# Moving two norms between the steps of a fused attention and mixture-of-experts block

## The chip, the cores and the metric

The kernel runs on one core of one Trainium2 chip. The metric is the device time of one execution in microseconds (us); three runs of the kernel before gave 756.25, 756.53 and 757.11. The engines are named as in the profile: PE (TensorE, matrix multiplies), DVE (VectorE), ACT (ScalarE), POOL (GpSimd) and SP (SyncE, which here only issues transfers). Each runs its own instructions in the order written, and they meet at semaphores.

## The reference, cut to what matters

Eight sequences of 256 tokens with 256 features pass through one block. The six modulation vectors come from a small product of c. The attention has 16 query heads and 8 key/value heads of 128 features, rotary embedding, a two-tap causal convolution on keys and values, and a causal window of 128. The expert part has 32 experts, of which each token takes 4, and a shared expert.

```python
h = _layernorm(x, axis=-1) * (1 + ca) + sa          # the input norm
x = x + ga * _L0_attn_ref(h, W_pack, W_o, conv_k, conv_v)
h = _layernorm(x, axis=-1) * (1 + cb) + sb          # the residual's second norm
x = x + gb * _L0_ffn_ref(h, w_norm, w_router, w_gate, w_up, w_down, sw_gate, sw_up, sw_down, w_shared_gate)
```

`_L0_ffn_ref` begins with an RMS norm of its own, then router, experts and shared expert.

## The kernel before, in words

**Pairs and steps.** The sequences are taken two at a time: four pairs (0 to 3) of 512 tokens. The attention is one software pipeline of 128 steps, 32 for each pair. A step n is one head of one sequence. Each engine walks through the same steps (`for n in STEPS`), and in step n it does its share for several heads at once: PE does `scores(n)`, `weighted_v(n - 2)`, `output(n - 3)`, `p_transpose(n - 1)` and `project(n + 4)`; DVE does the masked scores of n, `head_low(n - 2)` (the low part oT_lo of a head's output), in every fourth step `k_conv` (kc), `project(n + 3)` and `normalise(n)` (prob); ACT does `project(n + 3)` (two half copies qsw, or one of v), `head_high(n - 2)`, the exponentials of n and the transposed probabilities of n - 1; POOL does the two rotary operations on the queries and keys. PE's `scores(n)` write one of three PSUM banks and wait for `ot_done` of n - 2, so for `head_low(n - 3)` (lines 1453 to 1465). In every fourth step PE also transposes v (`v_transpose`). In the text "step 7 of pair 2" is n = 2 x 32 + 7.

**Hooks.** At a step's end each engine calls `hooks(n)` (ACT line 635, DVE line 1184, PE line 1558), a table that puts side work of other stages at given steps l of the pair p now in the pipeline. There are two such stages, and both touch the change:

- *The input norm of the next pair*, q = p + 1. DVE takes mean and variance of the four token rows of xin (`prepare_stats`, two calls of two rows each), ACT the reciprocal root (`prepare_norm`, line 517), DVE normalises xin in place (`prepare_norm`, line 976, two calls), PE transposes it in two halves through the PSUM bank XB (`prepare_t`), ACT scales it into hst (`prepare_h`) and rounds the high part (`prepare_hi`), and DVE takes the low part (`prepare_lo`). PE's `project` for the next pair's first head then reads both. `v_transpose` uses the same bank XB, and in group 3 it waits until `prepare_h` is done (line 1473).
- *The end of the pair before*, p - 1 ("post" in the names). DVE gates its attention output (`post_gate`), POOL adds it to the residual (`post_x1`), DVE takes statistics (`post_stats`), ACT the root (`post_std`), DVE the modulated second norm h2 (`post_h2`, four instructions per call, line 1074), ACT its squares and their root (`post_squares`, `post_rms`), DVE the RMS norm (`post_xn`), and PE, ACT and DVE the transposes and the router behind it.

**The load of xin.** `prepare_stats` waits for xin with `ld_xin` (line 968). SP issues that load in `next_x` (line 380) as soon as the pair ahead has been transposed out of xin, but SP's queue is in order too. For pair 2 the load stands behind `pair_loads(0)` and behind three fills of the expert sums with zeros of 2176 KB each (line 424), which come after the modulation rows are done; for pair 3 it stands behind the stores of pair 0 and the loads of pair 1:

```python
            pair_loads(0)
            for d in acc_d:
                sp.dma_start(d.rearrange("(a p) h -> p a h", p=PN),
                             blank[:, 0:H].unsqueeze(1).broadcast_to([PN, B * S // PN + 1, H])).then_inc(st_accz, 16)
            for p in range(NPAIR - 1):
                if p + 2 < NPAIR:
                    next_x(p + 2)
```

After the 128 steps follow the shared expert and the 32 experts, which the change doesn't touch.

## Time and profile before

| What | Value |
|---|---|
| median of three runs | 756.53 us |
| the profiled execution: its own time | 757.21 us |
| the profiled execution: its span, first to last instruction | 755.4 us |
| PE busy | 727.5 us, 96% of the span |
| DVE, ACT, POOL busy | 70%, 62%, 57% |
| mean granted TensorE clock | 0.99 |
| the 128 steps | from 23.2 to about 544 us of the span |

The times in the views count from the span's first instruction. The profiled execution took 757.21 us, 1.8 more than its span, and is one of the slower executions by 0.68 against the median. A busy PE is not a PE at its peak: matmuls overlap, and their ends are modelled. What a row names behind "<-" in brackets is what ended the idle time before it.

### The profile page before, as it was taken

Reading aid. Unit: us, or ns where it says so; the run is one execution under the profiler, and the core shown is the slowest. Engines: PE = TensorE matmul, PEld = TensorE weight load, DVE = VectorE, ACT = ScalarE, POOL = GpSimd, SP = SyncE. Lnnn points to the kernel's source line nnn. Section 1 sums busy time; section 2 is a strip of 40 time slices with the busy share of each in tenths; the row PEclk is TensorE's granted clock in tenths of the full one; section 3 lists DMA queues with packets and bytes.
Section 4 is the critical chain, followed back from the end, with each engine's and each line's share of the span. In section 5 each row is a group of like instructions: output and inputs, shape, how many; then the busy total and the mean of one; then the engine's idle time right before and its main releaser. Section 6 shows DMA issues by size and latency. Waiting matters only on the chain.

```text
span 755.4 us, 12879 instructions
## 1 busy us (share of the span) xinstructions
PE 727.5 (96%) x4144; PEld 624.1 (83%) x4144; DVE 531.0 (70%) x1554; ACT 464.7 (62%) x1273; POOL 429.9 (57%) x339
## 2 busy tenths in 40 slices
PE   8799999999999999999999999999999989999996
PEld 6598889988899998889999888999877857777875
DVE  5898897689876868987686797778664225454383
ACT  5788868777986776788677678777553212222110
POOL 3545445454465588646548864655545507567356
PEclk9999999999999999999999999999999989999998
DMA  8960007600005011000401102040369889996772
GB/s 303 322 139 1 2 0 241 230 0 2 1 1 192 5 49 48 33 1 1 166 2 48 40 28 76 3 168 1 124 166 258 220 267 263 289 228 71 171 226 84
DMA packets 62418, 84.44 MB, mean 112 GB/s; under 512 B 6376, under 2 KB 50293, under 8 KB 62352
## 3 DMA queue, kind: packets, MB, share of 16 engines
q1 hardware_dynamic: 52240, 70.59, 30.4%
q0 software_dynamic: 7680, 8.95, 6.2%
q10 hardware_dynamic: 2432, 4.07, 1.5%
q8 instruction: 34, 0.56, 0.3%
q14 instruction: 32, 0.26, 0.1%
HBM read 54.81 MB, written 33.51 MB: 117 GB/s over the span
## 4 chain that ended last, share of the span: by engine, by line
PE 76%; DVE 12%; ACT 6%; issue 2%; DMA 2%; POOL 1%; ACTq 0%; POOLq 0%; DVEq 0%
PE PJ L1386 22%; PE OUT L1520 9%; PE U L1505 6%; PE U L1465 6%; PE U L1672 5%; PE U L1494 4%; PE U L1464 3%; PE U L1506 3%; PE U L1620 2%; PE U L1386 2%; PE XB L1691 2%; PE OUT L1691 2%; PE OUT L1620 2%; PE XB L1386 2%; ACT U L570 1%
## 5 line engine op out<-in xcount | busy, mean ns | idle before, releaser
L792 POOL TENSOR_TENSOR qsw<-qsw,sinT 128x512 f32<-128x512 f32 x95 | 125.7, 1323 | 167.4 <-ACT qsw L557 166.5
L1017 DVE CUSTOM_DVE_ANT_0 U<-U,mask 128x128 f32<-128x128 f32 (+1 forms) x256 | 86.6, 379 | 50.8 <-PE U L1465 50.4
L570 ACT ACTIVATE U<-U,nmax 128x128 f32<-128x128 f32 (+1 forms) x256 | 100.4, 392 | 32.0 <-DVE nmax L1017 31.5
L1386 PE MATMUL PJ<-hT_hi,w_hi 128*128 128x512 f32 x254 | 110.8, 436 | 1.1 <-issue 1.1
L1386 PE MATMUL PJ<-hT_lo,w_hi 128*128 128x512 f32 x254 | 100.4, 395 | 0.0
L1386 PE MATMUL PJ<-hT_hi,w_lo 128*128 128x512 f32 x254 | 100.2, 394 | 0.0
L796 POOL TENSOR_TENSOR qr<-qr,qsw 128x512 f32<-128x512 f32 x64 | 82.6, 1291 | 29.0 <-DVE qr L1001 28.4
L556 ACT ACTIVATE qsw<-PJ 64x512 f32<-64x512 f32 x96 | 57.1, 594 | 51.7 <-PE PJ L1386 42.3
L803 POOL DMA_INDIRECT slot_rows<-xn,sidx x64 | 64.8, 1012 | 40.8 <-issue 13.1
L1520 PE MATMUL OUT<-wo_hi,oT_hi 128*128 128x256 f32 x256 | 82.9, 324 | 1.4 <-DVE wo_lo L1041 1.2
L1034 DVE TENSOR_TENSOR oT_lo<-U,oT_hi 128x256 fp32r<-128x256 f32 x128 | 54.1, 423 | 37.4 <-ACT oT_hi L577 37.2
L1505 PE MATMUL U<-pT,vN 128*128 128x256 f32 x256 | 77.2, 383 | 1.9 <-ACT pT L589 1.1
L1465 PE MATMUL U<-kc,qr 128*128 128x256 f32 x256 | 76.5, 380 | 0.0
L1027 DVE TENSOR_TENSOR prob<-U,rinv 128x384 f32<-128x384 f32 x128 | 71.3, 557 | 4.4
L896 POOL DMA_INDIRECT expert_sum<-ye,slot_token x32 | 49.7, 1553 | 41.6 <-DVE ye L1327 20.7
L1520 PE MATMUL OUT<-wo_hi,oT_lo 128*128 128x256 f32 x256 | 72.7, 284 | 0.0
L1520 PE MATMUL OUT<-wo_lo,oT_hi 128*128 128x256 f32 x256 | 71.5, 279 | 0.0
L577 ACT ACTIVATE oT_hi<-U 128x256 fp32r<-128x256 f32 x128 | 49.3, 386 | 34.0 <-PE U L1506 26.5
L1464 PEld LDWEIGHTS U<-kc,qr 128*128 128x128 f32 x256 | 46.6, 188 | 24.6 <-DVE oT_lo L1034 9.1
L589 ACT ACTIVATE pT<-U 128x384 f32<-128x384 f32 x128 | 63.4, 496 | 0.7 <-PE U L1494 0.7
L1494 PE MATMUL U<-ident,prob 128*128 128x128 f32 x384 | 62.9, 273 | 0.3 <-DVE prob L1027 0.3
L1464 PE MATMUL U<-kc,qr 128*128 128x128 f32 x256 | 50.8, 280 | 7.8 <-DVE oT_lo L1034 4.0
(227 smaller groups left out, 1837.1 us busy)
## 6 DMA issues: line engine op xcount, KB each, us to landing
wgu<-in_dram SPq DMA_DIRECT2D x32, 352.0 KB, 9.7
expert_sum<-blank SPq DMA_DIRECT2D x3, 2176.0 KB, 17.5
slot_rows<-blank SPq DMA_DIRECT2D x1, 4624.0 KB, 26.5
late_sums<-expert_sum SPq DMA_DIRECT2D x9, 512.0 KB, 8.9
wd_a<-in_dram SPq DMA_DIRECT2D x12, 352.0 KB
wraw<-in_dram SPq DMA_DIRECT2D x8, 512.0 KB, 8.7
bcm<-mod_rows SPq DMA_DIRECT2D x8, 512.0 KB, 6.8
xe<-slot_rows ACTq DMA_DIRECT2D x10, 289.0 KB, 6.7
```

Of the source, the lines that this page charges most:

```text
L570: last = act.activation(U[n % 3][:, a:z], U[n % 3][:, a:z], ACT.Exp, scale=-1.0, bias=nmax[:, n % 4, j:j + 1], accum_out=rsum[:, n % 4, j: ...
L792: pool.tensor_tensor(pair3(qsw[:, n % NQSW, :]), pair3(qsw[:, n % NQSW, :]), both(sinT[:, :]), ALU.mult).then_inc(t2_done, 1)
L796: pool.tensor_tensor(rope_buffer(m), rope_buffer(m), qsw[:, n % NQSW, :], ALU.add).then_inc(rope_done, 1)
L803: pool.indirect_dma_start(out=slots_d, out_offset=bass.IndirectOffsetOnAxis(ap=sidx[:, c:c + 1], axis=0), in_=xn[:, p % 2, c // TOPK, :], ...
L1017: last = dve.tensor_tensor_reduce(out=U[n % 3][:, a:z], in0=U[n % 3][:, a:z], in1=allowed, scale=-float(HD) ** -0.5, scalar=3.4e38, op0=AL ...
L1027: dve.tensor_tensor(prob[:, n % 2, :].rearrange("p (j k) -> p j k", k=PN), U[n % 3][:, 0:3 * PN].rearrange("p (j k) -> p j k", k=PN), rinv ...
L1386: last = pe.matmul(out_ap, a(c), b_(c), start=(n == 0), stop=(n == len(steps) - 1))
L1464: pe.matmul(U[n % 3][:, 0:PN], q[:, 0:PN], k[:, 0:PN], start=True, stop=True)
L1465: pe.matmul(U[n % 3][:, PN:3 * PN], q[:, PN:S], k, start=True, stop=True).then_inc(sc_ps, 1)
L1494: last = pe.transpose(U[n % 3][:, j * PN:(j + 1) * PN], prob[:, n % 2, j * PN:(j + 1) * PN], ident[:, :])
L1505: pe.matmul(o, v[:, 0:PN], pT[:, n % 2, 0:S], start=True, stop=False)
L1520: last = pe.matmul(OUT[b][:, t * H:(t + 1) * H], o, w[:, head, :], start=(head == 0 and t == 0 and i == 0), stop=(head == NH - 1 and i == ...
```

## The change

The function `turn(q)` gives the step of pair q - 1 at which the transposes of pair q's xin begin: 10 for pair 1 as before, 6 for pairs 2 and 3. For q = 2 and 3 the statistics of xin stood in steps 0 and 3 of pair q - 1, ACT's root in step 4 and DVE's normalising in steps 5 and 8; they move to steps 26 and 28 (statistics), 29 (root) and 30 (first half of the normalising) of pair q - 2 and to step 0 of pair q - 1 (second half). Pair 1's stay. `v_transpose` waits for `prepare_h` in group 2 instead of 3 for these pairs. The low part of the input norm moves from steps 16 and 19 to 14 and 17 (all pairs). Of the end of the pair before: the statistics, both in step 4, are split over 4 and 5, the root moves from step 5 to 6, h2 from 6 and 7 to 8 and 9, the squares from 7 and 8 to 9 and 10, their root from 9 to 11, the RMS norm from 11 and 12 to 12 and 13. No instruction is added or removed, and SP's and POOL's programs stay as they are.

```diff
--- before.py
+++ after.py
@@ -347,6 +347,10 @@
             p, l = divmod(n, UNITS)
             return p + 1, l
 
+        def turn(q):
+
+            return 10 if q == 1 else 6
+
         STEPS = range(-LEAD, NU + 3)
         block = ctx.enter_context(nc.Block())
 
@@ -637,19 +641,21 @@
                 q, _ = next_step(n)
                 if n < 0 or n >= NU:
                     return
-                if l == 4 and q < NPAIR:
+                if l == 4 and q == 1:
                     prepare_norm(q)
-                if l == 5 and p >= 0:
+                if l == 29 and q + 1 < NPAIR:
+                    prepare_norm(q + 1)
+                if l == 6 and p >= 0:
                     post_std(p, 0, 2)
                 if q < NPAIR:
-                    if l in (10, 11):
-                        prepare_h(q, l - 10, XB)
+                    if l - turn(q) in (0, 1):
+                        prepare_h(q, l - turn(q), XB)
                     if l in (13, 15):
                         prepare_hi(q, (l - 13) // 2)
                 if p >= 0:
-                    if l in (7, 8):
-                        post_squares(p, l - 7)
-                    if l == 9:
+                    if l in (9, 10):
+                        post_squares(p, l - 9)
+                    if l == 11:
                         post_rms(p)
                     if l in (14, 17):
                         post_xnt(p, (l - 14) // 3)
@@ -1184,23 +1190,30 @@
             def hooks(n):
                 p, l = post_step(n)
                 q, _ = next_step(n)
-                if q < NPAIR:
+                if q == 1:
                     if l in (0, 3):
                         prepare_stats(q, l // 3)
                     if l in (5, 8):
                         prepare_norm(q, (l - 5) // 3)
-                    if l in (16, 19):
-                        prepare_lo(q, (l - 16) // 3)
+                if q + 1 < NPAIR:
+                    if l in (26, 28):
+                        prepare_stats(q + 1, (l - 26) // 2)
+                    if l == 30:
+                        prepare_norm(q + 1, 0)
+                if q < NPAIR:
+                    if l == 0 and q > 1:
+                        prepare_norm(q, 1)
+                    if l in (14, 17):
+                        prepare_lo(q, (l - 14) // 3)
                 if p >= 0:
                     if l in (1, 2):
                         post_gate(p, l - 1)
-                    if l == 4:
-                        post_stats(p, 0)
-                        post_stats(p, 1)
-                    if l in (6, 7):
-                        post_h2(p, l - 6)
-                    if l in (11, 12):
-                        post_xn(p, l - 11)
+                    if l in (4, 5):
+                        post_stats(p, l - 4)
+                    if l in (8, 9):
+                        post_h2(p, l - 8)
+                    if l in (12, 13):
+                        post_xn(p, l - 12)
                     if l in (15, 18):
                         post_xnt(p, (l - 15) // 3)
                     if l == 21:
@@ -1470,7 +1483,7 @@
                 pe.wait_ge(pj_dve, 4 * G + 3)
                 if G >= 1:
                     pe.wait_ge(vn_done, G)
-                if g == 3 and p + 1 < NPAIR:
+                if p + 1 < NPAIR and g == turn(p + 1) // 4 + 1:
                     pe.wait_ge(ht_used, ht_scaled(p + 1, HC - 1))
                 if g == 4:
                     if p > 0:
@@ -1560,10 +1573,10 @@
                 q, _ = next_step(n)
                 v_out = n // 4 + 1
                 if q < NPAIR:
-                    if l == 10:
+                    if l == turn(q):
                         pe.wait_ge(vn_done, v_out)
                         prepare_t(q, 0, XB)
-                    if l == 11:
+                    if l == turn(q) + 1:
                         pe.wait_ge(ht_used, ht_scaled(q, 0))
                         prepare_t(q, 1, XB)
                 if p < 0 and l in MOD_STEPS:
```

How this stands in the built programs, first on DVE at steps 26 and 27 of pair 0. L1017 (L1023 in the change) are the masked scores, L1027 (L1033) is prob, L1034 (L1040) oT_lo, L1010 kc. Before:

```order
L1027 TENSOR_TENSOR prob<-U,rinv 128x384 [waits rinv_done]
L1017 ISA U,nmax<-U,mask 128x128 [waits sc_ps]
L1017 ISA nmax 128x1
L1017 ISA U,nmax<-U,mask 128x256
L1017 ISA nmax 128x1
L1034 TENSOR_TENSOR oT_lo<-U,oT_hi 128x256 [waits ot_hi_done]
L1010 SCALAR_TENSOR_TENSOR kc<-kr,cwk,k 128x512 [waits k0_done]
```

In the change, at the same place:

```order
L1033 TENSOR_TENSOR prob<-U,rinv 128x384 [waits rinv_done]
L976 BN_STATS st<-xin 128x6 [waits ld_xin]
L976 BN_STATS st<-xin 128x6
L979 BN_AGGR mv<-st 128x2 [waits dve_own]
L979 BN_AGGR mv<-st 128x2
L1023 ISA U,nmax<-U,mask 128x128 [waits sc_ps]
L1023 ISA nmax 128x1
L1023 ISA U,nmax<-U,mask 128x256
L1023 ISA nmax 128x1
L1040 TENSOR_TENSOR oT_lo<-U,oT_hi 128x256 [waits ot_hi_done]
```

Pair 2's statistics (st, mv), with their wait for the load of xin, now stand between prob of step 26 and the scores of step 27, and oT_lo behind them.

Second, DVE in pair 1: the first half of h2 (L1080 and L1084; L1086 and L1090 in the change). Before, at the end of step 6:

```order
L1027 TENSOR_TENSOR prob<-U,rinv 128x384 [waits rinv_done]
L1080 SCALAR_TENSOR_TENSOR h<-xres,mv,bcm 128x256 [waits rstd2_done]
L1080 SCALAR_TENSOR_TENSOR h<-xres,mv,bcm 128x256
L1084 SCALAR_TENSOR_TENSOR h<-h,rstd,bcm 128x256 [waits dve_own]
L1084 SCALAR_TENSOR_TENSOR h<-h,rstd,bcm 128x256
L1017 ISA U,nmax<-U,mask 128x128 [waits sc_ps]
L1017 ISA nmax 128x1
L1017 ISA U,nmax<-U,mask 128x256
L1017 ISA nmax 128x1
L1034 TENSOR_TENSOR oT_lo<-U,oT_hi 128x256 [waits ot_hi_done]
L1010 SCALAR_TENSOR_TENSOR kc<-kr,cwk,k 128x512 [waits k0_done]
```

In the change, at the end of step 8:

```order
L1033 TENSOR_TENSOR prob<-U,rinv 128x384 [waits rinv_done]
L1086 SCALAR_TENSOR_TENSOR h<-xres,mv,bcm 128x256 [waits rstd2_done]
L1086 SCALAR_TENSOR_TENSOR h<-xres,mv,bcm 128x256
L1090 SCALAR_TENSOR_TENSOR h<-h,rstd,bcm 128x256 [waits dve_own]
L1090 SCALAR_TENSOR_TENSOR h<-h,rstd,bcm 128x256
L1023 ISA U,nmax<-U,mask 128x128 [waits sc_ps]
L1023 ISA nmax 128x1
L1023 ISA U,nmax<-U,mask 128x256
L1023 ISA nmax 128x1
L1040 TENSOR_TENSOR oT_lo<-U,oT_hi 128x256 [waits ot_hi_done]
L1007 TENSOR_TENSOR kr<-PJ,cosT 128x512 [waits pj_act]
```

The same four instructions have moved by two steps: the step that follows was one with kc and vT, and is now one with a rotary product (kr).

## Rows read from the trace of the kernel before

**Rows 1.** The page, part 1: busy us (share of the span) and instructions of each engine.

```profile
PE 727.5 (96%) x4144; PEld 624.1 (83%) x4144; DVE 531.0 (70%) x1554; ACT 464.7 (62%) x1273; POOL 429.9 (57%) x339
```

**Rows 2.** Windows: two quiet steps of pair 0. Length, busy us (instructions) of each engine, clock, DMA.

```profile
129.74:133.49 3.75, 3.75 (x25) 3.38 (x24) 2.40 (x8) 3.37 (x9) 2.57 (x3) 1.00 1.09 380
137.23:141.42 4.19, 4.19 (x29) 3.81 (x27) 3.00 (x11) 3.27 (x9) 2.38 (x2) 1.00 1.08 384
```

**Rows 3.** Windows: steps 7 to 10 of pairs 1, 2 and 3.

```profile
179.89:198.12 18.23, 16.98 (x101) 13.98 (x100) 16.12 (x44) 14.26 (x46) 8.03 (x7) 1.00 0.01 1
312.26:330.79 18.53, 16.99 (x101) 13.99 (x100) 16.40 (x44) 14.28 (x46) 10.21 (x10) 1.00 0.04 17
444.93:462.34 17.41, 16.54 (x97) 13.55 (x96) 14.28 (x41) 13.32 (x43) 9.17 (x9) 1.00 0.03 8
```

**Rows 4.** Timeline of DVE, pair 2, steps 5 to 8: start, us, instruction.

```profile
309.19 1.10 DVE L981 TENSOR_SCALAR xin<-xin,mv,rstd 128x256 f32<-128x256 f32 x2
310.20 0.29 DVE L1017 CUSTOM_DVE_ANT_0 U<-U,mask 128x128 f32<-128x128 f32 x1
...
312.60 1.71 DVE L1080 SCALAR_TENSOR_TENSOR h<-xres,mv,bcm 128x256 f32<-128x256 f32 x2
...
315.14 0.29 DVE L1017 CUSTOM_DVE_ANT_0 U<-U,mask 128x128 f32<-128x128 f32 x1
...
318.07 0.87 DVE L1080 SCALAR_TENSOR_TENSOR h<-xres,mv,bcm 128x256 f32<-128x256 f32 x2
...
320.81 0.28 DVE L1017 CUSTOM_DVE_ANT_0 U<-U,mask 128x128 f32<-128x128 f32 x1
```

**Rows 5.** Timeline of SP's queue: issues around the loads of xin.

```profile
118.82 13.20 SPq L425 DMA_DIRECT2D expert_sum<-blank  x3
132.07 6.65 SPq L383 DMA_DIRECT2D xin<-in_dram  x1
...
238.52 0.67 SPq L383 DMA_DIRECT2D xin<-in_dram  x1
```

**Rows 6.** The tile xin on SP, 130 to 150 us: from issue to landing.

```profile
DMA to landing us min/median/max: 12.9/12.9/12.9
```

**Rows 7.** Timeline of DVE: pair 0, steps 26 and 28; pair 1, steps 3, 4 and 8.

```profile
132.80 0.56 DVE L1027 TENSOR_TENSOR prob<-U,rinv 128x384 f32<-128x384 f32 x1
...
138.09 0.30 DVE L1017 CUSTOM_DVE_ANT_0 U<-U,mask 128x128 f32<-128x128 f32 x1 [0.26 <-PE U L1465]
...
169.25 0.74 DVE L970 BATCH_NORM_STATS2 st<-xin 128x6 f32<-128x256 f32 x2
...
170.19 0.27 DVE L1017 CUSTOM_DVE_ANT_0 U<-U,mask 128x128 f32<-128x128 f32 x1
...
188.15 0.29 DVE L1017 CUSTOM_DVE_ANT_0 U<-U,mask 128x128 f32<-128x128 f32 x1
```

**Rows 8.** Timeline of PE: pair 0, step 28; pair 1, step 9.

```profile
137.23 0.38 PE L1464 MATMUL U<-kc,qr 128*128 128x128 f32 x2
...
137.89 0.59 PE L1505 MATMUL U<-pT,vN 128*128 128x256 f32 x2
...
189.21 0.49 PE L1464 MATMUL U<-kc,qr 128*128 128x128 f32 x2 [0.53 <-DVE oT_lo L1034]
...
190.26 0.70 PE L1505 MATMUL U<-pT,vN 128*128 128x256 f32 x2
```

**Rows 9.** Timeline of PE behind the pair loop.

```profile
572.58 4.52 PE L1620 MATMUL U<-swd,hs 128*128 128x256 f32 x12
...
600.86 2.76 PE L1620 MATMUL U<-swd,hs 128*128 128x256 f32 x12
...
612.20 1.13 PE L1662 MATMUL PJ<-ident,xe 128*128 128x128 f32 x4 [3.40 <-DMA xe<-slot_rows]
```

**Rows 10.** Windows: the two stretches with the lower granted clock.

```profile
573.42:576.83 3.41, 3.41 (x10) 2.69 (x9) 3.10 (x22) 0.37 (x2) 0.00 (x0) 0.50 0.91 218
611.00:617.80 6.80, 5.51 (x13) 3.51 (x14) 1.71 (x8) 0.32 (x1) 0.00 (x0) 0.50 1.01 352
```

## The prediction

> **What bounds the kernel now.** On the page, TensorE (PE) is busy for 727.5 us, 96% of the span, where VectorE (DVE) has 70%, ScalarE (ACT) 62% and GpSimd (POOL) 57% [rows 1]. So almost every microsecond is a TensorE microsecond, and an edit on another engine counts only where TensorE waits for it. The windows view shows a step at its floor: 3.75 us, or 4.19 us where four 128-column transposes are added, with TensorE busy throughout [rows 2]. Against these floors I read steps 7 to 10 of pairs 1, 2 and 3 [rows 3]. In pairs 1 and 2 two of the four steps carry transposes: 2 x 3.75 + 2 x 4.19 = 15.88 us is the floor, and they took 18.23 and 18.53. In pair 3 there is no next pair to transpose: floor 15.44, taken 17.41. Lost: 2.35 + 2.65 + 1.97 = 6.97 us.
>
> DVE's timeline shows why [rows 4]. A step's own DVE work, from its first score instruction to its hook, takes 2.40 us (310.20 to 312.60). On top of it the normalising of two rows of xin adds 1.01 (309.19 to 310.20), the first half of h2 2.54 (312.60 to 315.14), the second 2.74 (318.07 to 320.81). Step 6 then lasts 4.94 us on DVE and step 7 5.67, and TensorE, which needs DVE's oT_lo of three steps back for its next scores, waits. (Step 3 of pairs 2 and 3 has a loss of its own, k_conv behind POOL's post_x1; the change leaves both where they are.)
>
> **The change part by part.** *The new wait.* Pair 2's statistics move from step 0 of pair 1 to step 26 of pair 0, six steps earlier, and they wait for the load of xin for pair 2. SP issues this load at 132.07, behind the three fills of expert_sum that start at 118.82 [rows 5], and it lands 12.9 us after its issue, at 144.97 [rows 6]. The change touches nothing in SP's order, and nothing before that point that SP waits for, so the load lands at the same time. DVE reaches the new place when the normalise of step 26 ends, at 132.80 + 0.56 = 133.36 [rows 7]. It stands there for 11.6 us. Behind it in DVE's queue are the scores of step 27 (ACT's exps wait for them) and head_low(25). TensorE can finish step 27, whose inputs are complete, and stops at the scores of step 28, which began at 137.23 [rows 8] and need head_low(25). After the landing DVE needs 0.94 for the statistics (169.25 to 170.19 [rows 7]), then starts its scores, and TensorE follows 1.06 after that start (188.15 to 189.21 [rows 7, 8]): 144.97 + 0.94 + 1.06 = 146.97, which is 9.74 late. The weighted_v of that step starts 2.11 after DVE's scores (188.15 to 190.26), at 148.02, where it would follow TensorE's scores by 0.66 (137.23 to 137.89), at 147.63 [rows 7, 8]: 0.39 more. **Stall: 10.1 us**; bounds 9.7 (no second wait) and 10.7 (the next step also waits). TensorE is the bound, so none of it is made up later.
>
> The load for pair 3 has no such wait: issued at 238.52 [rows 5], it is there at 251.4 even with the same 12.9 us, and step 26 of pair 1 begins at least 15 x 3.75 us after 198.12 [rows 3], at 254.4 or later.
>
> *The clock.* TensorE stands still for 9.7 us. After an idle time of 3.40 us before 612.20 [rows 9], the granted clock is 0.50, that is 1.2 GHz, from 611.00 to 617.80, still 5.6 us after work began again [rows 10]. In the other low stretch, 573.42 to 576.83, twelve matmuls took 4.52 us and not 2.76 [rows 9, 10]: 1.76 us lost in 3.41. I expect the lower level when work resumes at 147, for a time between these two, so between 1.76 and half of 5.6, 2.8. **Clock: 2.3 us**, the middle; bounds 0 (no row excludes that it stays up) and 3.4 (half of the whole 6.8).
>
> The Trainium skill (TensorE: Matmul & The Clock Gate, Terms) prices such a time at its length times one less the granted share; by that price the 6.8 us stretch costs 3.4, an estimate, and the forecast would be 1.1 higher. In this trace part of that stretch had no work in it, so the row with work decides.
>
> *The gain.* Pairs 1 and 2 lose two statistics (0.94 each) and the two normalisings (1.01 each) from steps 0 to 8, one normalising coming back in step 0, where the statistics had stood without loss. The second norm's statistics are split over steps 4 and 5, and h2 comes to steps 8 and 9. So DVE enters step 8 in time and has there 2 x 2.40 + 2.54 + 2.74 = 10.08 us of work for 4.19 + 3.75 = 7.94 of TensorE: 2.14 late. In a quiet step DVE starts 0.86 us after TensorE's scores (137.23 to 138.09 [rows 7, 8]) and the next scores may follow 1.06 after DVE, so 3.75 - 0.86 - 1.06, about 1.8 us of lateness is free and 0.3 is not; with weighted_v's 2.11 in place of 0.66 it is 0.7, and the k_conv of step 11, whose result step 12 needs, adds some 0.2. **I take 0.9 lost per pair.** Bounds: 0 (all of it forgiven) and 1.97, what pair 3 lost with h2 alone [rows 3]; I stay below it because pair 3 came to h2 already late, with all four statistics of its second norm in step 4, two of them 0.94. Gain: 6.97 - 3 x 0.9 = **4.3 us**; bounds 1.1 and 7.0.
>
> *At nothing.* The statistics in steps 26 and 28 and half a normalising in steps 30 and 0: 2.40 + 0.94 or 2.40 + 1.01 fits in 3.75. Without that cover (a late DVE) each would cost up to its 1 us. The xin transposes (now in steps 6 and 7) cost TensorE the same 0.44 wherever they stand. The ACT work that comes with them (prepare_h, and post_std in step 6) falls into a step with up to 3.37 us of ACT work [rows 2]; it may run past the end of step 6, and step 7, where ACT has one copy of v and not the two of qsw, takes it up. Without that cover oT_hi would come late by as much. The later squares, post_rms, post_xn and prepare_lo have their consumers moved with them or several steps away. SP and POOL keep their order, so no DMA is issued at another place in it.
>
> **Sum**, against the profiled execution's own 757.21 us: + 10.1 + 2.3 - 4.3 = 765.3. The median of the runs is 0.68 lower than that execution, so I forecast **764.6 us**, slower by 8.1.
>
> **The rivals.** (1) *The load is there in time.* Then only the gain is left: 756.5 - 4.3 = **752.2**, faster. It decides by one point: a landing before 133.4. For it speaks only that the fills' pace might change; against it, the row that puts the landing 11.6 us after that point. Chance 0.04. (2) *The new steps 8 and 9 are as crowded as 6 and 7 were*: h2 in two neighbouring steps, POOL's rope additions beside it, ACT's squares behind it, each pair losing the 1.97 of pair 3. Gain 1.1, time 756.5 + 10.1 + 2.3 - 1.1 = **767.8**. For it: h2's 2.54 and 2.74 will not shrink by moving. Against it: no late entry from step 4. Chance 0.15. (3) *Everything is forgiven and the clock stays up*: 756.5 + 10.1 - 7.0 = **759.6**. For it: 3.75 - 2.40 leaves DVE 1.35 us in each quiet step; against it, the clock's fall after 3.40 us of idle. Chance 0.08. (4) *TensorE has more to do ahead of the block than I count* or the load's landing moves by several microseconds, so that stall and gain about cancel: no change. Chance 0.03. (5) *The lower clock covers work for the whole 6.8 us* of the longer stretch: 3.4 in place of 2.3, **765.7**, a matter of size inside the forecast's own range. For it: the idle time here is three times as long; against it: both rows with work show less. Chance 0.15. My forecast keeps 0.55.
>
> **How the numbers follow.** The range holds the forecast and rivals 2 and 5 and ends just above rival 3: from 760 (stall 9.7, clock 0.8, gain 7.0) to 769 (10.7 + 2.9 - 1.1). About 0.2%, 1.5 us, is what a measurement of this kernel can tell from no change. Slower by more than that are the forecast and rivals 2, 3 and 5: 0.93; faster is rival 1: 0.04; the rest, 0.03, is within it.
>
> **What the changed profile would show.** A wait of DVE's xin statistics for the DMA of about 11.6 us ending near 145, once; TensorE's longest wait for oT_lo near 9.5 us in the same place; a granted clock of 0.50 just behind it; steps 7 to 10 of each pair near their floor and steps 8 to 12 about 0.9 over it; step 3 of pairs 2 and 3 unchanged. The prediction is wrong if the statistics of pair 2 start near 133.5, if the stall is there but pair 1 begins less than 9 us late, or if steps 8 to 12 lose as much as steps 7 to 10 did.

## The result and the profile after

The changed kernel takes **768.59 us** (median of five runs, 767.64 to 771.18) where the kernel before, run again beside it, took 756.53; the ratio is 1.0156, 95% interval 1.0131 to 1.0181. The forecast was 764.6 with a range of 760 to 769: the sign and the range hold, the size is 4 us short. The profiled execution is the slowest of the five, 771.18 us with a span of 769.4 and a mean granted clock of 0.981, and 13.97 above the profiled execution before.

Page of the change, part 1: the busy times have grown by little, so the new time is waiting and clock [rows 1].

```profile
PE 733.1 (95%) x4144; PEld 629.5 (82%) x4144; DVE 538.2 (70%) x1554; ACT 464.2 (60%) x1273; POOL 429.8 (56%) x339
```

View of waits, change, 125 to 165 us: the engine and line that waited, for what, total us, times, longest.

```profile
DVE st L976 <- DMA xin<-in_dram: 11.3, 1, 11.3
...
PE U L1477 <- DVE oT_lo L1040: 9.9, 1, 9.9
```

Windows of the change: pair 0's steps 27 and 28, and the stretch of the lower clock, columns as in [rows 2].

```profile
133.44:147.29 13.85, 3.92 (x25) 3.22 (x23) 2.67 (x11) 2.08 (x7) 0.62 (x1) 0.83 0.76 259
147.29:154.23 6.94, 6.94 (x28) 6.31 (x28) 4.63 (x16) 3.75 (x10) 2.54 (x2) 0.60 0.00 0
142.66:152.90 10.24, 5.61 (x22) 5.28 (x23) 6.80 (x24) 4.16 (x13) 2.35 (x2) 0.50 0.07 23
```

DVE stood 11.3 us (forecast 11.6), TensorE 9.9. Step 27 took 13.85 where 3.75 is its floor [rows 2]: **10.1 us, as in the sum**. That it agrees to the tenth is luck, as DVE's and TensorE's timelines show (start, us, instruction):

```profile
144.58 0.75 DVE L976 BATCH_NORM_STATS2 st<-xin 128x6 f32<-128x256 f32 x2 [11.27 <-DMA xin<-in_dram]
...
145.53 0.27 DVE L1023 CUSTOM_DVE_ANT_0 U<-U,mask 128x128 f32<-128x128 f32 x1
...
146.44 0.74 DVE L1016 SCALAR_TENSOR_TENSOR kc<-kr,cwk,k 128x512 f32<-128x512 f32 x1
```

```profile
147.29 0.77 PE L1477 MATMUL U<-kc,qr 128*128 128x128 f32 x2 [9.93 <-DVE oT_lo L1040]
```

The load landed 0.4 us earlier than forecast. TensorE then followed DVE's scores by 1.76 us and not by 1.06: step 28 is one of the fourth steps, whose `scores` also wait for kc (`kc_done`), and kc ends at 147.18, 0.65 after the oT_lo that the view names. The second wait of 0.39 that the sum counts isn't in this step, and the three differences cancel. Step 28 took 6.94 for 4.19, at a granted clock of 0.60: 2.75 us, where 2.3 stood in the sum.

The gain did not come. Windows of steps 6 to 12 of pairs 1 to 3 in the kernel before (its steps 7 to 10 are [rows 3]):

```profile
176.14:206.50 30.36, 29.11 (x179) 25.00 (x177) 26.68 (x76) 25.05 (x75) 13.94 (x11) 1.00 0.00 1
308.50:339.17 30.67, 29.13 (x179) 25.01 (x178) 26.97 (x76) 25.06 (x75) 16.91 (x14) 1.00 0.04 16
441.17:470.28 29.11, 28.24 (x171) 24.13 (x169) 23.85 (x70) 22.71 (x68) 16.21 (x14) 1.00 0.12 40
```

The same seven steps in the change:

```profile
188.91:218.77 29.86, 28.77 (x179) 25.15 (x177) 24.69 (x71) 24.61 (x74) 13.48 (x11) 1.00 0.00 1
320.97:350.83 29.86, 28.78 (x178) 25.15 (x177) 24.68 (x71) 24.47 (x74) 16.45 (x14) 1.00 0.04 16
454.63:483.60 28.97, 27.88 (x170) 24.27 (x169) 24.68 (x71) 22.76 (x70) 16.44 (x14) 1.00 0.13 44
```

The floor of these seven steps is 3 x 3.75 + 4 x 4.19 = 28.0 us in pairs 1 and 2 (two with the transposes of xin, two of v) and 27.1 in pair 3. Lost before: 2.4, 2.7, 2.0. Lost in the change: 1.9, 1.9, 1.8, and now in steps 10 and 11 (4.67 and 4.61 in every pair). The seven steps gained 1.45 us in the three pairs together; steps 13 to 20 of pairs 1 and 2 grew by 0.47 together. That leaves a gain of 1.0 where the sum had 4.3.

DVE's timeline in the change, pair 1, steps 8, 9 and 11 (start, us, instruction), shows h2 (first half, second half) and a late oT_lo:

```profile
200.83 1.52 DVE L1086 SCALAR_TENSOR_TENSOR h<-xres,mv,bcm 128x256 f32<-128x256 f32 x2
202.39 0.88 DVE L1090 SCALAR_TENSOR_TENSOR h<-h,rstd,bcm 128x256 f32<-128x256 f32 x2
...
205.59 1.31 DVE L1086 SCALAR_TENSOR_TENSOR h<-xres,mv,bcm 128x256 f32<-128x256 f32 x2
206.93 1.98 DVE L1090 SCALAR_TENSOR_TENSOR h<-h,rstd,bcm 128x256 f32<-128x256 f32 x2
...
213.32 0.42 DVE L1040 TENSOR_TENSOR oT_lo<-U,oT_hi 128x256 fp32r<-128x256 f32 x1 [1.36 <-ACT oT_hi L581]
```

POOL's timeline beside the second half of h2:

```profile
204.94 1.28 POOL L802 TENSOR_TENSOR kr<-kr,qsw 128x512 f32<-128x512 f32 x1 [0.53 <-DVE kr L1007]
207.35 1.28 POOL L798 TENSOR_TENSOR qsw<-qsw,sinT 128x512 f32<-128x512 f32 x1 [1.13 <-ACT qsw L561]
```

The second half of h2 (205.59 to 208.84) now takes 3.25 us, where [rows 4] had 2.74: both of its instruction pairs stand beside a POOL operation, and a pair that takes 0.88 without one takes 1.31 and 1.98. Then, in step 11, oT_lo waits 1.36 for ACT. ACT's timeline from the end of step 10 says why:

```profile
210.78 0.73 ACT L568 ACTIVATE k<-kr,cwk 128x512 f32<-128x512 f32 x1
211.39 0.42 ACT L617 ACTIVATE yg<-h 128x256 f32<-128x256 f32 x1
...
212.33 0.69 ACT L553 ACTIVATE v<-PJ,cwv 128x512 f32<-128x512 f32 x1
212.91 0.38 ACT L581 ACTIVATE oT_hi<-U 128x256 fp32r<-128x256 f32 x1
```

At step 10's end ACT has k_tap (L568) and the moved squares (L617) ahead of oT_hi of step 11, all behind exponentials that were already late. DVE's kc of that step, for which the scores of step 12 wait, stands behind the late oT_lo.

A third thing was in no step of the prediction. Windows of the change, steps 21 and 22 (the router logits) of pairs 1 and 2:

```profile
250.96:261.12 10.16, 10.16 (x71) 9.44 (x70) 5.75 (x22) 6.17 (x19) 4.69 (x5) 1.00 0.72 217
383.01:394.79 11.78, 11.78 (x72) 10.64 (x71) 5.75 (x22) 6.18 (x19) 4.70 (x5) 0.86 0.47 141
```

With the same work and TensorE busy throughout, pair 2's took 1.62 us more, since the granted clock was at 0.50 for 3.4 us from 388.4; pair 3's (from 521.5) took 1.6 more too. The profile before has no such stretch in the 128 steps. Other executions do, the kernel before with its load moved up among them (experiment 2). The account: 10.1 + 2.75 - 1.0 + 3.2, and 1.0 us less behind the last step, make 14.05; measured 13.97. Between the medians lie 12.06 us, and the first three terms alone make 11.85.

The last pair's logits, behind the 128 steps, are of the same 34-column matmuls, and in each of the 14 traces the clock falls to 0.50 during them or within 0.9 us behind them, there with short idle times of TensorE among them. In the kernel before that is the first stretch of [rows 10], from 573.42. The timeline there:

```profile
572.47 0.26 PE L1386 MATMUL XB<-wr_hi,xnT_lo 128*128 128x34 f32 x1
```

### The profile page after: what moved, and what is told of

Its sections match the earlier page's. It is cut to its first block, busy times and chain, and to the rows that moved or that the text cites. A ratio compares the mean times of both kernels' runs of the same rounds, so it can differ in the third digit from the quotient of the medians.

```text
span 769.4 us, 12878 instructions
## 1 busy us (share of the span) xinstructions
PE 733.1 (95%) x4144; PEld 629.5 (82%) x4144; DVE 538.2 (70%) x1554; ACT 464.2 (60%) x1273; POOL 429.8 (56%) x339
## 4 chain that ended last, share of the span: by engine, by line
PE 78%; DVE 8%; ACT 5%; DMA 3%; issue 2%; SPq 2%; POOL 1%; ACTq 0%; POOLq 0%; DVEq 0%
PE PJ L1399 22%; PE OUT L1533 10%; PE U L1518 6%; PE U L1478 6%; PE U L1685 5%; PE U L1507 5%; PE U L1477 3%; PE U L1519 3%; PE U L1633 2%; PE U L1399 2%; PE XB L1704 2%; PE OUT L1704 2%; PE OUT L1633 2%; PE XB L1399 2%; SPq L429 2%
## 5 line engine op out<-in xcount | busy, mean ns | idle before, releaser
L1023 DVE CUSTOM_DVE_ANT_0 U<-U,mask 128x128 f32<-128x128 f32 (+1 forms) x256 | 86.6, 380 | 46.8 <-PE U L1478 45.8
L1040 DVE TENSOR_TENSOR oT_lo<-U,oT_hi 128x256 fp32r<-128x256 f32 x128 | 54.2, 423 | 37.8 <-ACT oT_hi L581 36.6
L1033 DVE TENSOR_TENSOR prob<-U,rinv 128x384 f32<-128x384 f32 x128 | 71.4, 558 | 4.4
```

The lines of the kernel that those rows point to most:

```text
L1023: last = dve.tensor_tensor_reduce(out=U[n % 3][:, a:z], in0=U[n % 3][:, a:z], in1=allowed, scale=-float(HD) ** -0.5, scalar=3.4e38, op0=AL ...
L1033: dve.tensor_tensor(prob[:, n % 2, :].rearrange("p (j k) -> p j k", k=PN), U[n % 3][:, 0:3 * PN].rearrange("p (j k) -> p j k", k=PN), rinv ...
```

## The experiments

**1. The load ahead of the fills.** SP issues pair 2's xin right behind `pair_loads(0)`. The diff is made to the change.

```diff
             pair_loads(0)
+            next_x(2)
             for d in acc_d:
                 ...
-                if p + 2 < NPAIR:
+                if p > 0 and p + 2 < NPAIR:
                     next_x(p + 2)
```

> The changed kernel with one transfer moved: the load of xin for pair 2 is issued before the three fills of expert_sum and not behind them. Theory (the early statistics wait for this load, and the wait is the whole loss): DVE's statistics of pair 2 no longer wait, step 27 of pair 0 takes 3.75 us and not 13.85, step 28 takes 4.19 and not 6.94, so 12.8 us go and the time is about 768.6 - 12.8 = 755.8, within 1.5 us of the kernel before. Rival (the loss is in the new places of the hooks, the wait only shows it first): the time stays above 762.

758.15 us against 757.88 for the kernel before on that chip, ratio 0.9999 (0.9972 to 1.0026). Windows of steps 27 and 28 of pair 0:

```profile
133.81:137.55 3.74, 3.74 (x24) 3.38 (x23) 3.34 (x12) 2.26 (x7) 0.63 (x1) 1.00 1.09 384
137.55:141.74 4.19, 4.19 (x28) 3.82 (x27) 3.50 (x13) 3.26 (x9) 2.38 (x2) 1.00 1.09 385
```

They are back at their floors; steps 6 to 12 take 29.87, 29.85 and 28.96, as in the change. So the wait and its clock are the whole slowdown, and without them the rest of the change is worth nothing that can be measured: the expected gain of 4.3 us, 0.57%, is not there. (The time of 755.8 was worked out from the first result; on this chip the kernel before took 757.88 and not 756.53, so the ratio is what counts.) This run's profile had the low clock behind the logits in all three pairs.

**2. The same load order in the kernel before.** The edit of experiment 1, made to the kernel before.

> The kernel before with the load of xin for pair 2 issued before the three fills. In the kernel before, the statistics stand in pair 1, some 11 us after the load has landed, so theory: no change, 756.5 within 0.7. Rival (the order of load and fills matters for something else, so that the gain of the first run would not be the wait's): over 1 us away.

758.09, ratio 0.9995 (0.9969 to 1.002): the early load alone is worth nothing that can be measured, so the runs below that have it may be compared with the kernel before.

**3. The statistics alone.** The kernel before, with only the statistics of xin of pairs 2 and 3 moved.

```diff
-                if q < NPAIR:
-                    if l in (0, 3):
-                        prepare_stats(q, l // 3)
+                if q == 1 and l in (0, 3):
+                    prepare_stats(q, l // 3)
+                if q + 1 < NPAIR and l in (26, 28):
+                    prepare_stats(q + 1, (l - 26) // 2)
```

> The kernel before with only the statistics of xin for pairs 2 and 3 moved to steps 26 and 28 of the pair ahead; root, normalising, transposes, h2 and all else as before. Theory (the wait comes with this one move): stall 10.1 and slow clock 2.7 as in the changed kernel; steps 3 to 10 of pairs 1 and 2 get 1.9 us less DVE work each and lose perhaps 0.5 to 1.5 less per pair, so 756.5 + 12.8 - 2 = 767.3, between 766 and 769. Rival (the stall needs the other moves too): at or below 757.

768.78, ratio 1.015 (1.0103 to 1.0197); windows of steps 27 and 28 of pair 0:

```profile
133.79:148.02 14.23, 3.91 (x24) 3.22 (x23) 2.67 (x11) 2.08 (x7) 0.63 (x1) 0.76 0.78 270
148.02:153.86 5.84, 5.84 (x27) 5.21 (x28) 4.36 (x14) 3.71 (x10) 2.56 (x2) 0.72 0.00 0
```

The statistics alone, with their wait, moved by six and seven steps, bring the whole slowdown: 10.5 and 1.65 us here, 10.1 and 2.75 in the change. The clock's share is smaller since its stretch at 0.50 lay from 141.07 to 151.31, so that 3.3 us of it were left when TensorE resumed at 148.02, where the change had 5.6 left (147.29 to 152.90). About half of what was left is the loss both times.

**4. TensorE kept at work during the wait.** The change, with 20 extra matmuls into a scratch bank ahead of the scores of step 28.

```diff
+                if n == 28:
+                    pe.wait_ge(vn_done, 7)
+                    for _ in range(20):
+                        pe.matmul(XB[:, 0:S], ident[:, :], cosT[:, :], start=True, stop=True)
                 if 0 <= n < NU:
                     scores(n)
```

> The changed kernel with twenty extra 256-column matmuls on TensorE in front of the scores of step 28 of pair 0, where it would stand still; they write a bank that is overwritten before it is read. Theory (2.75 us of the loss come from the lower clock after the idle time): the granted clock stays 1.0 through the stall, step 28 takes about 4.2 us and not 6.94, and the time falls by 2.75 to about 765.8. Rival (step 28 is long because DVE and ACT refill the pipeline): step 28 stays near 6.9 and the time near 768.6.

766.72, ratio 1.0114 (1.0067 to 1.0161). Windows of steps 27 and 28 in this run; the clock is the third number from the right:

```profile
134.11:147.94 13.83, 12.55 (x65) 10.82 (x63) 2.67 (x11) 2.08 (x7) 0.63 (x1) 1.00 0.77 270
147.94:152.20 4.26, 4.26 (x27) 3.89 (x28) 4.04 (x14) 3.58 (x10) 2.38 (x2) 1.00 0.00 0
```

Step 27 kept its 13.83 us, step 28 took 4.26 at the full clock. So 2.68 of the 2.75 us were the clock, and without the idle time it did not fall. The medians do not separate this run from the change; the two windows do.

**5. The input norm alone.** As experiment 1, with the residual's second norm back at its old steps.

```diff
-                    if l in (4, 5):
-                        post_stats(p, l - 4)
-                    if l in (8, 9):
-                        post_h2(p, l - 8)
+                    if l == 4:
+                        post_stats(p, 0)
+                        post_stats(p, 1)
+                    if l in (6, 7):
+                        post_h2(p, l - 6)
...
```

The root, the squares and the RMS norm go back likewise; their lines, and the early load of experiment 1, are left out here.

> The changed kernel with the load of xin for pair 2 issued ahead of the three fills, and with the residual's second norm put back to its old steps (statistics 4, root 5, h2 6 and 7, squares 7 and 8, RMS norm 11 and 12): the first half of the change alone, without its stall. Steps 6 to 12 take 30.36, 30.66 and 29.11 us in pairs 1 to 3 of the kernel before and 29.87, 29.85 and 28.97 with the whole change and the early load. Theory (h2 loses about 2 us a pair wherever its two halves stand in neighbouring steps, so the second half of the change brought nearly nothing): 30.0, 30.0 and 29.1, time within 0.2% of the kernel before. Rival (the move of h2 carried the gain): pairs 1 and 2 stay at 30.4 and 30.7.

754.44 against 758.11, ratio **0.9966** (0.9945 to 0.9986). Both expectations were wrong. Windows of steps 6 to 12, pairs 1 to 3:

```profile
176.05:204.07 28.02, 28.02 (x179) 25.28 (x178) 22.89 (x70) 24.42 (x72) 13.25 (x11) 1.00 0.00 1
307.87:335.97 28.10, 28.10 (x178) 25.23 (x177) 22.98 (x70) 24.42 (x72) 16.27 (x14) 1.00 0.04 17
438.23:467.35 29.12, 28.24 (x170) 24.12 (x169) 23.84 (x70) 22.73 (x68) 16.22 (x14) 1.00 0.12 41
```

Pairs 1 and 2 run at their floor with h2 where it always stood; pair 3, with the same second norm and no transposes of xin, loses 2.0 as before. The change's first half takes 4.9 us out of the seven steps of pairs 1 and 2, and its second half puts 3.6 back there.

**6. Why steps 6 and 7 can take h2.** Experiment 5, with the transposes of xin back at steps 10 and 11.

```diff
-            return 10 if q == 1 else 6
+            return 10
```

> The run with the input norm's half alone, and the transposes of xin put back to steps 10 and 11 for all pairs (statistics and normalising stay in the pair ahead, h2 in steps 6 and 7). That half alone brought steps 6 to 12 of pairs 1 and 2 to 28.0 and 28.1 us, their floor, and left pair 3, which has no transposes, at 29.1. Theory (the 0.44 us of transposes in each of steps 6 and 7 are TensorE work that covers DVE's h2 in the same steps): with the transposes in steps 10 and 11 pairs 1 and 2 lose what pair 3 loses, 30.0 us each, and the time is about that of the kernel before. Rival (xin's normalising in steps 5 and 8 was the whole loss): the two pairs stay at 28.1, time 3.5 us below the kernel before.

757.33 against 758.34, ratio 0.9989 (0.9967 to 1.0012). Windows of steps 6 to 12 in this run:

```profile
176.37:206.31 29.94, 29.13 (x179) 25.01 (x178) 24.06 (x70) 24.44 (x72) 13.30 (x11) 1.00 0.00 1
308.51:338.54 30.03, 29.14 (x179) 25.02 (x177) 24.16 (x70) 24.44 (x72) 16.28 (x14) 1.00 0.04 16
440.79:469.89 29.10, 28.25 (x171) 24.12 (x170) 23.83 (x70) 22.71 (x68) 16.20 (x14) 1.00 0.12 40
```

The loss is back, 1.9 and 2.0, as expected. The transposes in steps 6 and 7 cover h2. By the timelines they do it in two ways, which no run separates: TensorE has 0.88 us more to do in those steps, and ACT's prepare_h puts off its qsw copies and with them POOL's next operation, from 186.42 here to 187.03 in experiment 5, so that h2's last pair of instructions, from 186.09, takes 1.91 us here and 0.88 there (from 185.79).

Of xin's own part only the statistics brought a gain. With them alone moved (experiment 3) the seven steps of pairs 1 and 2 took 29.91 and 29.99; with the root and the normalising moved too, as here, 29.94 and 30.03. The two normalisings, 1.01 us of DVE work each, cost nothing in steps 5 and 8 once the statistics were gone.

**7. ACT's lag.** Experiment 1, with the second half of the squares moved on to step 11.

```diff
-                    if l in (9, 10):
-                        post_squares(p, l - 9)
+                    if l in (9, 11):
+                        post_squares(p, (l - 9) // 2)
```

> The changed kernel with the early load and with the second half of the squares moved on ACT from step 10 to step 11, where ACT has one copy of v and not two half copies. Theory (step 11's 4.6 us come from ACT, which in step 10 does k_tap and squares before oT_hi): step 11 falls to 4.0 or below, step 10 stays at 4.66, steps 6 to 12 at 29.2 and 28.3 (pairs 1 and 2, pair 3), time 1.5 to 2 us below the run with the early load alone. Rival (step 11 is late because h2's second half, 3.25 us on DVE, is late): step 11 stays at 4.6 and the sums at 29.9 and 29.0.

757.04 against 758.11, ratio 0.9983 (0.996 to 1.0007). Step 11 fell from 4.61 to 4.25, not to the 4.0 expected, and step 10 stayed at 4.67; the seven steps took 29.42, 29.40 and 28.52. Window of pair 1:

```profile
176.00:205.42 29.42, 28.54 (x179) 25.25 (x178) 24.38 (x71) 24.51 (x74) 13.09 (x11) 1.00 0.00 1
```

So ACT's squares were 0.45 of the 1.85 lost per pair, about half of what steps 11 and 12 lost. The rest goes with DVE's late h2, as experiment 8 shows. The median does not separate this run from the kernel before; the windows do.

**8. h2 in four pieces.** Experiment 7, with the first products in steps 6 and 7 and the second in 8 and 9.

```diff
-                    if l in (8, 9):
-                        post_h2(p, l - 8)
+                    if l in (6, 7):
+                        post_h2(p, l - 6, (0,))
+                    if l in (8, 9):
+                        post_h2(p, l - 8, (1,))
```

The new argument of `post_h2` picks the first or the second products; its own lines are left out here.

> As the run with the later squares, and h2 is cut into four pieces of two instructions: the first products of both halves in steps 6 and 7, the second ones in steps 8 and 9. Theory (DVE's crowding in two neighbouring steps is the loss of step 10): no step has more than 2.0 us of h2, step 10 falls from 4.66 to 4.0 or below, steps 6 to 12 of pairs 1 and 2 take 28.6 (floor 28.0), pair 3 27.7, time 3 to 4 us below the run with the early load alone, about 754. Rival (the loss is POOL's rope additions, which hold up h2's instructions wherever they stand in steps 8 and 9): step 10 stays above 4.3, sums 29.0.

752.69 against 758.11, ratio **0.993** (0.9906 to 0.9954). Windows of steps 6 to 12; all three pairs stand on their floors, pair 3 too, lower than the 28.6 and 27.7 expected:

```profile
176.15:204.14 27.99, 27.99 (x178) 25.40 (x177) 24.29 (x71) 24.64 (x74) 12.95 (x11) 1.00 0.00 1
308.03:336.01 27.98, 27.98 (x178) 25.40 (x177) 24.39 (x71) 24.49 (x74) 15.94 (x14) 1.00 0.05 17
438.26:465.37 27.11, 27.11 (x171) 24.53 (x169) 23.94 (x71) 22.98 (x70) 15.96 (x14) 1.00 0.13 44
```

DVE's work in the seven steps is hardly less than in experiment 1 (24.29 against 24.65 us); it is spread. POOL still stretches a piece to 1.5 us, but that fits into a step.

**9. h2 in POOL's gaps.** Experiment 1, with h2's halves in steps 6 and 10, the root in step 5 and the squares in 7 and 11.

```diff
-                    if l in (8, 9):
-                        post_h2(p, l - 8)
+                    if l in (6, 10):
+                        post_h2(p, l // 10)
...
```

> The changed kernel with the early load, and h2's halves in steps 6 and 10, in the two places where POOL has no rope work for some 5 us (root in step 5, squares in steps 7 and 11). Theory (POOL's additions stretch h2's halves from 1.75 us to 2.4 and 3.2, and two neighbouring steps cannot take them): each half takes 1.8 us, no step from 6 to 12 is more than 0.3 over its floor, sums 28.4 and 27.5, time 4 us below the run with the early load alone, about 754. Rival (POOL doesn't matter, DVE's own 2.4 us a step and the h2 of a whole half are too much for one step): steps 7, 8 and 11, 12 lose 0.5 each, sums 29.4 or more.

754.85, ratio 0.996 (0.9936 to 0.9984), but not as thought: the sums are 28.74, 28.73 and 28.70, so pair 3 lost 1.6; neither the theory's sums nor the rival's came. Step 7 of pair 3 took 5.0. ACT's timeline at the end of step 5 there:

```profile
441.68 0.20 ACT L611 ACTIVATE rstd<-mv 128x4 f32<-128x4 f32 x1 [1.52 <-DVE mv L1078]
```

I had put ACT's root into the step whose DVE hook makes the second statistics; ACT stood 1.52 us, and DVE's oT_lo of step 6 then waited 1.42 for oT_hi: the change's own mistake in small. Nor was the first half free of POOL (its first pair took 1.51).

**10. POOL's additions apart.** Experiment 8, with the two `post_x1` in steps 2 and 3 and not both in 3.

```diff
-                    if l == 3:
-                        post_x1(p, 0)
-                        post_x1(p, 1)
+                    if l in (2, 3):
+                        post_x1(p, l - 2)
```

> As the run with h2 in four pieces, and POOL's two residual additions, both in step 3, are placed in steps 2 and 3. In step 3 of pairs 2 and 3 k_conv takes 2.71 us on DVE beside them, and 0.74 in step 7; step 3 lasts 5.08 us there against 3.77 in pair 1. Theory (DVE's k_conv is held up while POOL adds, for as long as both additions stand together): step 3 falls to 4.4 us or below, time 1 to 2.5 us below the run with h2 in four pieces. Rival (the second addition alone still meets k_conv, or the first one delays the rope work of the next step): step 3 stays above 4.7, or step 2 or 4 takes over the loss.

748.29 against 758.34, ratio **0.988** (0.984 to 0.992): more than expected. POOL's timeline in experiment 8, step 3 of pair 2 (line numbers shift by a few between the kernels):

```profile
296.81 2.52 POOL L819 TENSOR_TENSOR xres<-xres,yg 128x512 f32<-128x512 f32 x2
```

DVE's there:

```profile
297.18 2.71 DVE L1017 SCALAR_TENSOR_TENSOR kc<-kr,cwk,k 128x512 f32<-128x512 f32 x1
```

POOL's here, with the additions in steps 2 and 3:

```profile
294.41 1.28 POOL L819 TENSOR_TENSOR xres<-xres,yg 128x512 f32<-128x512 f32 x1
...
296.87 1.29 POOL L819 TENSOR_TENSOR xres<-xres,yg 128x512 f32<-128x512 f32 x1
```

And DVE's k_conv here:

```profile
296.00 0.74 DVE L1016 SCALAR_TENSOR_TENSOR kc<-kr,cwk,k 128x512 f32<-128x512 f32 x1
```

k_conv now falls between the two additions and takes 0.74; step 3 of pairs 2 and 3 fell from 5.08 to 3.75. That is 1.33 twice; the rest of the 4.4 us between the medians is not accounted for by steps. In the two profiled executions 1.6 more is the clock behind pair 1's logits in experiment 8, and 3.2 lie behind the 128 steps, where experiment 8 had two stretches of 6.8 us at 0.50 and this run one.

**11. The logits cut up.** Experiment 8, with the 24 narrow matmuls in four groups between the projection's wide ones.

```diff
+            def logits_and_project(p, m):
...
+                for i, (wt, x, c) in enumerate(pairs):
+                    last = pe.matmul(PJ[m % 2][:, :], wt[j][:, c, cols], x, start=(i == 0), stop=(i == 5))
...
+                    if i % 2 == 1:
+                        done = logits_of(i // 2 + 1)
```

> As the run with h2 in four pieces, and TensorE's 24 matmuls of 34 columns for the router logits in step 21, which ran in one piece of 2.7 us, are cut into four groups of six with two projection matmuls of 512 columns between each two groups. The granted clock falls to 0.50 for 3.4 us behind these logits in some of the three pairs of most executions seen so far, and steps 21 and 22 then take 1.6 us more than 6.42 + 3.75. Theory (the stretch of narrow matmuls lets the clock fall): no stretch at the lower clock in any of the three pairs, steps 21 and 22 take 10.2 us in all of them, the median is 1.5 to 3 us below the run with h2 in four pieces (about 750.5), and the runs spread less. Rival (the fall is not due to them, or to their number and not their order): it appears as often as before and the time is the same.

752.27, ratio 0.9919 (0.9888 to 0.9949), not to be told from experiment 8. Steps 21 and 22 took 10.17 us in all three pairs at the full clock, as expected, but the kernel before and experiments 3, 6 and 10 had no fall in theirs either. Over the twelve traces with the logits in one piece the fall is in 16 of 36 such stages, and four traces have none. Inconclusive.

**12. The last two together.** Experiments 10 and 11 in one; on TensorE the cut takes the place of a projection:

```diff
+                if 0 <= n < NU and p >= 0 and l == 21:
+                    pe.wait_ge(vn_done, n // 4 + 1)
+                    logits_and_project(p, n + LEAD)
-                if n + LEAD < NU:
+                elif n + LEAD < NU:
                     project(n + LEAD)
```

> The two last edits together: h2 in four pieces, POOL's additions in steps 2 and 3, and the router's narrow matmuls cut into four groups between projection matmuls. The run with the additions split had no stretch of low clock in steps 21 in its profiled execution, but its executions lie between 745.2 and 753.4 us, median 748.3. Theory (some of those executions have the clock's fall at the logits, and the cut prevents it): no low clock in steps 21 of the profiled execution, highest of the runs below 751, median 746 to 747. Rival (the cut does nothing for the clock; what spreads the runs is elsewhere, behind the 128 steps): median 748 to 749 and as wide a spread.

747.62 against 757.56, ratio **0.9871** (0.9846 to 0.9896), between 745.98 and 748.82; all three pairs again at the full clock in steps 21 and 22. The five runs have mean clocks of 0.988 to 0.992, two of the six of experiment 10 had 0.981 and 0.983, at 753.4 and 752.8. It points to the theory, but so few runs do not show it; the medians of the two cannot be told apart, and 747.62 lies above the 746 to 747 expected. This version and experiment 10's beat both kernels.

## Why the prediction was right, and where not

- *The stall* held in cause and size, not step by step: 10.1 as forecast, with a landing 0.4 early, a wait for kc that was in no step of the prediction (0.7) and no second wait (0.39). Experiments 1 and 3 show that it is the load's place behind the fills, with the wait moved in front of it, that makes the change slower.
- *The clock* held in kind (experiment 4) and nearly in size: 2.75 for 2.3. The price by the whole 6.8 us, 3.4, was too high, the price of the row with work a little low. Experiment 3 lost 1.65 behind the same wait, so the size varies with the place of the stretch.
- *The gain is the step that failed*: "I take 0.9 lost per pair". Measured: 1.85, near rival 2's figure (1.97), so the gain was 1.0 for 4.3 and the time, 768.59, came near rival 2's 767.8. The 3.3 us that the gain lacks and the 0.45 of the clock make 3.75 of the 4.0 by which the forecast was short; the wide range, which had rival 2 in it, is why it held.

Three things were wrong in the 0.9. First, DVE's lateness. DVE came to step 8 in time, as forecast, but to step 10 later. TensorE's and DVE's first scores of step 10 in the change, pair 1, and TensorE's of step 11:

```profile
205.22 0.38 PE L1477 MATMUL U<-kc,qr 128*128 128x128 f32 x2
...
208.84 0.28 DVE L1023 CUSTOM_DVE_ANT_0 U<-U,mask 128x128 f32<-128x128 f32 x1
...
209.90 0.49 PE L1477 MATMUL U<-kc,qr 128*128 128x128 f32 x2 [0.76 <-DVE oT_lo L1040]
```

That is 3.62 us behind TensorE where 0.86 is a quiet step's: 2.76 late, and 2.14 stood in the prediction. The second half of h2 was taken at 2.74 and became 3.25 behind POOL; and DVE's own work, taken at 2.40, is 2.68 in step 8, where a DVE that is in time first waits 0.33 for oT_hi. The first half came out 0.2 shorter. The prediction's rule for what lateness is free was right: TensorE again followed by 1.06, and step 10 lost the 0.9 that 2.76 gives by it, not 0.3.

Second, ACT's squares stood at nothing ("have their consumers moved with them or several steps away") and cost 0.45 (experiment 7).

Third, the reason for staying below pair 3's 1.97, "because pair 3 came to h2 already late", was false in the trace before. TensorE's and DVE's first scores in step 6 of pair 3, whose hook is the first half of h2:

```profile
441.17 0.38 PE L1464 MATMUL U<-kc,qr 128*128 128x128 f32 x2
...
442.02 0.30 DVE L1017 CUSTOM_DVE_ANT_0 U<-U,mask 128x128 f32<-128x128 f32 x1 [0.95 <-PE U L1465]
```

DVE was there 0.85 behind TensorE, after an idle time: as in a quiet step. So pair 3 already showed what h2 in two neighbouring steps costs with no late entry.

- *At nothing* stood too "the xin transposes ... cost TensorE the same 0.44 wherever they stand". True, and the point was missed: the work that they bring is cover. The change moved them to steps 6 and 7, where they would have hidden h2, and moved h2 away in the same edit (experiments 5, 6).
- *Not in the sum*: the clock behind the logits, 3.2 us of the profiled execution, which lies 2.6 above the median. Whether the other four executions had less of it is not shown, as only one was profiled. In the 78 recorded executions of the kernel before that stood beside the experiments, time goes with the mean granted clock: 761.8 to 764.9 us at 0.984, 754.8 to 758.7 at 0.992. Where the clock fell in each is not on record.

The prediction's own sign of being wrong, "if steps 8 to 12 lose as much as steps 7 to 10 did", nearly came in pair 3: 1.84 for 1.97. In pairs 1 and 2 it was 1.85 and 1.86 for 2.35 and 2.65.

## What to carry to other kernels

Before side work is moved ahead, follow its input to the queue that brings it: one early wait on an in-order engine cost 10 us, as much as the best version here won. When two pieces move at once, ask which of them was the other's cover, and try each alone: half of this change, without its wait, was a gain of 0.34%, and the other half gave it back. When a wait names one semaphore, look for another that came later: step 28 waited for kc and not only for oT_lo. And work that overfills two steps is better cut into pieces that each fit into a step's slack than moved to two other steps.

## What the runs showed of the hardware

A POOL operation holds up some DVE instructions: kc took 0.74 us alone and 2.71 beside two additions of 1.26 each, and ended 0.56 after them; h2's pairs of instructions took 0.88 and up to 1.98. The Trainium skill (SBUF — State Buffer, SBUF: two separate sides) says that, of a DVE instruction with two SBUF inputs and a GpSimd instruction that reads SBUF, the one that starts first holds the shared ports for its whole length and the other blocks; kc's row, which starts 0.37 after the additions and outlasts them, agrees.

The granted clock fell to 0.50 for 3.4 us with TensorE without idle time, behind 24 matmuls of 34 columns that took 2.8 us, in 16 of 36 such stages of twelve traces, at 1.6 us each. What decides when it falls stays open.

During 9.9 us without work the granted clock fell to 0.50 in the change, for 10.2 us, 5.6 of them with work, and the step behind it took 6.94 us for 4.19; with filler matmuls in the gap it stayed at 1.00, and the step took 4.26.
